# Quantising on a Trainium2 core: two bit operations in one VectorE pass, and a maximum moved to GpSimd

## What is computed

```
def fp4_quant_dequant(x):                       # BLOCK = 16
    scale = max(max(abs(block)) / 6, 1e-12)
    xn = block / scale
    idx = searchsorted([0.25, 0.75, 1.25, 1.75, 2.5, 3.5, 5.0], abs(xn))
    return [0, 0.5, 1, 1.5, 2, 3, 4, 6][idx] * sign(xn) * scale

h = layernorm(x) * (1 + ca) + sa
x = x + ga * attention(h)
h = layernorm(x) * (1 + cb) + sb
gate, up = fp4_linear(h, w_gate), fp4_linear(h, w_up)      # 256 -> 704
x = x + gb * fp4_linear(silu(gate) * up, w_down)           # 704 -> 256
```

## Time and profile before

| | |
|---|---|
| median of 3 runs | 4182.7 us (4179.85 to 4183.4) |
| the profiled execution, its own time | 4182.51 us |
| its span in the profile | 4180.7 us |
| TensorE (PE) busy | 3731.8 us, 89% |
| VectorE (DVE) busy | 3130.8 us, 75% |
| ScalarE (ACT) busy | 1946.8 us, 47% |
| GpSimd (POOL) busy | 1196.2 us, 29% |
| mean granted TensorE clock | 0.967 of full |

### The profile page before, as it was taken

One profiled execution on the slowest core, in us unless ns is written; L12 is line 12 of the kernel. 1 busy time (PEld: TensorE's weight loads), 2 busy tenths in 40 slices (PEclk: granted clock), 3 DMA queues, 4 the chain that ended last, 5 costly groups with the idle time before them and its releaser, 6 DMA issues.

```text
span 4180.7 us, 58634 instructions
## 1 busy us (share of the span) xinstructions
PE 3731.8 (89%) x22068; PEld 1974.5 (47%) x22068; DVE 3130.8 (75%) x6125; ACT 1946.8 (47%) x3535; POOL 1196.2 (29%) x886
## 2 busy tenths in 40 slices
PE   1799999999989989999999999999999998999886
PEld 0334454454545445454544545445454544544445
DVE  7477768778786787877777786777877688776855
ACT  2255444544444554444444454454544455445441
POOL 2222314132231323223132331423224132321223
PEclk6799999999999999999999999999999999999997
DMA  2532122213122122212213122222212212212000
GB/s 76 71 57 33 39 43 45 40 34 51 30 48 45 28 46 41 49 34 46 43 29 52 34 44 46 37 41 37 51 31 52 46 25 49 41 27 45 11 15 10
DMA packets 127981, 169.89 MB, mean 41 GB/s; under 512 B 22020, under 2 KB 75988, under 8 KB 127700
## 3 DMA queue, kind: packets, MB, share of 16 engines
...
...
## 4 chain that ended last, share of the span: by engine, by line
PE 73%; DVE 13%; ACT 9%; issue 2%; SPq 1%; DMA 1%; POOL 1%; DVEq 0%; ACTq 0%; POOLq 0%
PE o_acc L635 13%; PE banks L655 10%; PE banks L619 9%; PE banks L753 8%; PE banks L730 7%; PE banks L737 7%; ACT arena L815 7%; PE banks L686 4%; PE banks L711 3%; PE banks L694 3%; PE banks L746 2%; DVE banks L1020 2%; DVE tm L993 2%; PE banks L622 1%; PE banks L671 1%
## 5 line engine op out<-in xcount | busy, mean ns | idle before, releaser
L815 ACT ACTIVATE arena<-banks 128x512 f32<-128x512 f32 (+1 forms) x2432 | 1289.4, 576 | 1239.7 <-PE banks L622 702.9
L1020 DVE CUSTOM_DVE_ANT_0 banks<-banks,mask 128x640 f32<-128x640 f32 (+3 forms) x1024 | 1038.0, 1040 | 228.1 <-PE banks L655 218.3
L619 PE MATMUL banks<-qa,ka 105*128 105x512 bf16 (+3 forms) x3072 | 852.3, 332 | 154.3 <-ACT arena L815 125.4
L655 PE MATMUL banks<-ka,qa 102*128 102x512 bf16 (+3 forms) x3072 | 761.6, 334 | 104.7 <-DVE top L1020 80.1
L635 PE MATMUL o_acc<-arena,va 128*17 128x512 f32 (+3 forms) x6144 | 642.4, 500 | 13.1 <-ACT arena L815 12.5
L619 PEld LDWEIGHTS banks<-qa,ka 105*128 105x128 bf16 x3072 | 280.2, 98 | 674.1 <-ACT arena L815 471.2
L655 PEld LDWEIGHTS banks<-ka,qa 102*128 102x128 bf16 x3072 | 267.1, 99 | 484.8 <-DVE top L1020 150.9
L1018 DVE TENSOR_REDUCE top<-banks 128x2 f32<-128x768 f32 (+3 forms) x384 | 391.6, 1043 | 138.5 <-PE banks L660 107.8
L937 POOL TENSOR_TENSOR hid<-hid,tm 128x704 f32<-128x704 f32 x128 | 214.7, 1678 | 900.1 <-DVE hid L994 900.1
L753 PE MATMUL banks<-wdT,hqT 128*128 128x256 f32 x1536 | 371.2, 393 | 3.6 <-ACT hqT L846 3.2
L730 PE MATMUL banks<-wguT,xqT 128*128 128x352 f32 x1024 | 337.0, 463 | 2.8 <-ACT hqT L846 2.0
...
## 6 DMA issues: line engine op xcount, KB each, us to landing
...
```

The lines of the kernel that those rows point to most:

```text
L619: mm = pe.matmul(ps[:, m * w:(m + 1) * w], ka[g][0:KT, h, kt * P:(kt + 1) * P], qa[g][0:KT, h, q0:q0 + w], start=heads < G, stop=heads == ...
L655: mm = pe.matmul(ps[:, at:at + z - a], qa[g][0:KS, h0 + m, qt * P:(qt + 1) * P], ka[g][0:KS, h0 + m, a:z], start=qt > 0, stop=qt == 0 or h ...
L815: nc.scalar.activation(probs[:, s % P_SLOTS, j * heads:(j + 1) * heads, 0:w], ps[:, 0:heads * w].rearrange("p (h q) -> p h q", h=heads), A ...
L1020: nc.vector.tensor_tensor_reduce(out=ps, in0=ps, in1=mask[:, S - w:S], scale=1.0, scalar=MASKED, op0=ALU.add, op1=ALU.max, accum_out=tops) ...
```

## The change

The constant m gets another form. The mask 0x40800000 keeps one bit of the exponent that says "2 or more" and its lowest bit; or-ing 0x0B400000 makes of them MAGIC * 2 for magnitudes of 2 to 4, MAGIC * 4 for 4 to 8, and a tiny number below 2. The greater of that and MAGIC is what L993 made before. VectorE no longer runs L993: the maximum is the first half of the pass that adds m, which becomes a scalar_tensor_tensor. GpSimd gets a pass of its own that takes the maximum (L937 after the change), and then the two that it had (L939 and L942). Scales are made negative, so that the difference is taken as m minus the tile. In SM, the two passes that were a tensor_scalar and a copy become scalar_tensor_tensors with a second input of zeros. The planned costs of SM, XQ and HQ change with them.

```
--- before.py
+++ after.py
@@ -237,7 +237,7 @@
                 last = ("PE", ("S", b, g, j))
                 n += heads * w
             old = ("MT", b, g - 1) if g else ("MT", b - 1, NG - 1)
-            p.add("DVE", ("SM", b, g), 1.5, due, ("DVE", ("S", b, g, NT - 1)), ("DVE", old))
+            p.add("DVE", ("SM", b, g), 0.85, due, ("DVE", ("S", b, g, NT - 1)), ("DVE", old))
             older = ("TOP", b, g - 2) if g >= 2 else ("TOP", b - 1, g + 2)
             pe(("MT", b, g), 0.1, due, ("DVE", ("SM", b, g)), ring="D", on="DVE", takes_cost=0.27, then=(("SP", older),))
             p.add("SP", ("TOP", b, g), 0.8, due - 30.0, ("DVE", ("MT", b, g)), lag=4.0)
@@ -294,8 +294,8 @@
             p.add("DVE", ("LN", b, r), 2.6, due, ("DVE", ("LR", b)), ("SP", ("FROW", b)), ("PE", ("XT", *pair(-2))),
                   ("DVE", ("HQ", *tile(2 * r - 3))))
             p.add("DVE", ("XR", b, r), 1.35, due + 2, ("DVE", ("LN", b, r)), ("DVE", ("XQ", *pair(-1))))
-            p.add("DVE", ("XQ", b, r), 2.75, due + 4, ("DVE", ("XR", b, r)), ring="Q")
-            p.add("POOL", ("XQ", b, r), 2.6, due + 6, ("DVE", ("XQ", b, r)), takes="Q")
+            p.add("DVE", ("XQ", b, r), 2.1, due + 4, ("DVE", ("XR", b, r)), ring="Q")
+            p.add("POOL", ("XQ", b, r), 3.15, due + 6, ("DVE", ("XQ", b, r)), takes="Q")
             pe(("XT", b, r), 0.55, due + 8, ("POOL", ("XQ", b, r)), ("PE", ("UP", *tile(2 * r - 3))),
                ring="A", on="ACT", takes_cost=0.59)
             for t in (2 * r, 2 * r + 1):
@@ -308,8 +308,8 @@
                 pe(("UP", b, t), 2.4, late + 2, ("PE", ("GA", b, t, 1)), ("PE", ("UP", *tile(t - 1))), ring="D", on="DVE",
                    takes_cost=0.95, banks=2, then=(("ACT", ("GA", b, t, 1)),))
                 p.add("DVE", ("HR", b, t), 1.75, late + 4, ("DVE", ("UP", b, t)), ("DVE", ("HQ", *tile(t - 1))))
-                p.add("DVE", ("HQ", b, t), 3.15, late + 6, ("DVE", ("HR", b, t)), ring="Q")
-                p.add("POOL", ("HQ", b, t), 3.4, late + 8, ("DVE", ("HQ", b, t)), takes="Q")
+                p.add("DVE", ("HQ", b, t), 2.6, late + 6, ("DVE", ("HR", b, t)), ring="Q")
+                p.add("POOL", ("HQ", b, t), 4.15, late + 8, ("DVE", ("HQ", b, t)), takes="Q")
                 for k in range(2):
                     pe(("HT", b, t, k), 0.55 if k == 0 else 0.3, late + 12, ("POOL", ("HQ", b, t)),
                        ("PE", ("HT", b, t, 0)) if k else None, ("PE", ("DN", *tile(t - 2))), ring="A", on="ACT",
@@ -391,7 +391,7 @@
         mv, rs = ([sb(f"{n}{k}", shape) for k in range(2)] for n, shape in (("mv", [P, T, 2]), ("rs", [P, T])))
         ve, tn = sb("ve", [P, T]), sb("tn", [P, T])
         top = sb("top", [P, G * T])
-        top_rest = sb("top_rest", [P, G * T])
+        top_rest, zeros = sb("top_rest", [P, G * T]), sb("zeros", [P, G * T])
         top_parts = sb("top_parts", [P, 3, G * T], BF16)
         topT = [sb(f"topT{n}", [3 * G * T, P], BF16) for n in range(2)]
         rden = [sb(f"rden{n}", [P, T, G]) for n in range(2)]
@@ -934,8 +934,10 @@
                         u = (xb if kind == "XQ" else hid)[e[2] % 2][:, 0:w]
                         m, sc = tm[turn][:, 0:w], scales[kind[0]][e[2] % 2][:, :]
                         pool.wait_ge(rounded, done)
-                        nc.gpsimd.tensor_tensor(u, u, m, ALU.subtract).then_inc(gridded, 1)
-                        pool.wait_ge(gridded, done)
+                        nc.gpsimd.tensor_scalar(m, m, MAGIC, 1.0, ALU.max, ALU.mult).then_inc(gridded, 1)
+                        pool.wait_ge(gridded, 2 * done - 1)
+                        nc.gpsimd.tensor_tensor(u, m, u, ALU.subtract).then_inc(gridded, 1)
+                        pool.wait_ge(gridded, 2 * done)
                         blocks = u.rearrange("p (n k) -> p n k", k=BLOCK)
                         nc.gpsimd.tensor_tensor(blocks, blocks, sc.unsqueeze(2).broadcast_to((P, w // BLOCK, BLOCK)),
                                                 ALU.mult).then_inc(quant_done, 1)
@@ -981,24 +983,24 @@
             def block_scales(src, am, sc, iv):
 
                 step(nc.vector.tensor_reduce(am, blocks(src), AX.X, ALU.max, apply_absolute_value=True))
-                step(nc.vector.scalar_tensor_tensor(out=sc, in0=am, scalar=1.0 / 6.0, in1=tiniest[:, 0:am.shape[-1]],
-                                                    op0=ALU.mult, op1=ALU.max))
+                step(nc.vector.scalar_tensor_tensor(out=sc, in0=am, scalar=-1.0 / 6.0, in1=tiniest[:, 0:am.shape[-1]],
+                                                    op0=ALU.mult, op1=ALU.min))
                 step(nc.vector.reciprocal(iv, sc))
 
             def round_to_grid(u, iv, m):
 
-                step(nc.vector.scalar_tensor_tensor(out=blocks(u), in0=blocks(u), scalar=BELOW, in1=spread(iv),
+
+                step(nc.vector.scalar_tensor_tensor(out=blocks(u), in0=blocks(u), scalar=-BELOW, in1=spread(iv),
                                                     op0=ALU.mult, op1=ALU.mult))
-                step(nc.vector.tensor_scalar(m.bitcast(U32), u.bitcast(U32), 0x7F800000, None, ALU.bitwise_and))
-                step(nc.vector.tensor_scalar(m, m, 1.0, MAGIC, ALU.max, ALU.mult))
-                return nc.vector.tensor_tensor(u, u, m, ALU.add)
+                step(nc.vector.tensor_scalar(m.bitcast(U32), u.bitcast(U32), 0x40800000, 0x0B400000, ALU.bitwise_and, ALU.bitwise_or))
+                return nc.vector.scalar_tensor_tensor(out=u, in0=m, scalar=MAGIC, in1=u, op0=ALU.max, op1=ALU.add)
 
             def quantise(tile, n):
                 nb = n // BLOCK
                 m, am, sc, iv = tm[0][:, 0:n], amax["H"][:, 0:nb], scales["H"][0][:, 0:nb], inv["H"][:, 0:nb]
                 block_scales(tile, am, sc, iv)
                 step(round_to_grid(tile, iv, m))
-                step(nc.vector.tensor_tensor(tile, tile, m, ALU.subtract))
+                step(nc.vector.scalar_tensor_tensor(out=tile, in0=m, scalar=MAGIC, in1=tile, op0=ALU.max, op1=ALU.subtract))
                 return nc.vector.tensor_tensor(blocks(tile), blocks(tile), spread(sc), ALU.mult)
 
             def run():
@@ -1021,12 +1023,15 @@
                                                            op0=ALU.add, op1=ALU.max, accum_out=tops).then_inc(d_free, 1)
                     elif kind == "SM":
                         dve.wait_ge(d_free, in_d["S", b, e[2], NT - 1])
-                        step(nc.vector.tensor_scalar(top_parts[:, 0, :], top[:, :], -1.0, None, ALU.mult))
-                        step(nc.vector.scalar_tensor_tensor(out=top_rest[:, :], in0=top[:, :], scalar=-1.0, in1=top_parts[:, 0, :],
+                        part = [top_parts[:, n, :] for n in range(3)]
+                        step(nc.vector.scalar_tensor_tensor(out=part[0], in0=top[:, :], scalar=-1.0, in1=zeros[:, :],
+                                                            op0=ALU.mult, op1=ALU.add))
+                        step(nc.vector.scalar_tensor_tensor(out=top_rest[:, :], in0=top[:, :], scalar=-1.0, in1=part[0],
                                                             op0=ALU.mult, op1=ALU.subtract))
-                        step(nc.vector.tensor_copy(top_parts[:, 1, :], top_rest[:, :]))
-                        nc.vector.tensor_tensor(top_parts[:, 2, :], top_rest[:, :], top_parts[:, 1, :],
-                                                ALU.subtract).then_inc(top_ready, 1)
+                        step(nc.vector.scalar_tensor_tensor(out=part[1], in0=top_rest[:, :], scalar=1.0, in1=zeros[:, :],
+                                                            op0=ALU.mult, op1=ALU.add))
+                        nc.vector.scalar_tensor_tensor(out=part[2], in0=top_rest[:, :], scalar=1.0, in1=part[1],
+                                                       op0=ALU.mult, op1=ALU.subtract).then_inc(top_ready, 1)
                     elif kind == "MT":
                         g = e[2]
                         if g >= 2:
@@ -1136,7 +1141,8 @@
             step(nc.vector.memset(slope_row[:, 7, 1:6:2], 1.0))
             dve.sem_inc(tiny_set, 1)
             nc.vector.memset(va[:, :, :, HD:VW], 1.0)
-            nc.vector.memset(tiniest[:, :], 1e-12)
+            nc.vector.memset(tiniest[:, :], -1e-12)
+            nc.vector.memset(zeros[:, :], 0.0)
             step(nc.vector.memset(o_acc[:, :], 0.0))
 
             dve.wait_ge(pool_set, 4)
```

47 lines of the change are left out of this document (26 added, 21 removed).

## The result

The changed kernel takes 4264.1 us (median of 4, 4260.69 to 4268.89), beside 4181.27 us for the kernel before on the same chip. The ratio is 1.020, interval 1.018 to 1.022: about 2% slower. The forecast was 4151 us, with a range of 4112 to 4200.

The account below looks back on a forecast made before the run. TensorE, busy 89% of the span, was taken as the main bound, with waits for VectorE partly winnable. From 4182.5 us, terms of -22 - 5 + 0 + 1 - 3.5 - 2 + 0 = -31.5 us gave 4151 us, range 4112 to 4200.

Parts of the forecast that it names:

- term 4: GpSimd's added pass: 0.72 and 0.52 us each, mostly hidden behind attention work, bare in the tail: +1 us.
- Terms 1, 2: VectorE loses L993: -22 us where it collides with GpSimd's splittings, -5 us in the other 164 quantisations.
- term 5: Weights quantised ahead of the loop: eight tiles lose a pass of 0.3 to 0.53 us while TensorE waits: -3.5 us.
- Term 6: SM's two passes given a second input were to collide less with GpSimd: between 0 and -8 us, taken as -2.
- the two single places: Two quantisations beside GpSimd splittings in a batch: removing L993 was to win 0.44 us in one, 1.13 in the other.
- I take all of it: The mean win of 0.8 us at 28 collisions, -22 us, counted in full towards the kernel's time.
- rival B: TensorE is the bound: VectorE's freed time turns idle, only the weights' 3.5 us stay; 4179 us, chance 0.17.
- Term 7: New planned costs move GpSimd's splittings of units 2 and 3 in the lists: about 0, bounds -41 and +55 us.
- Rival C: Unit 2's splitting, moved ahead of tile 2, stalls VectorE's rounding there every batch, a third collision: 4206 us, chance 0.17.
- The signs to look for: Profile checks: GpSimd's new pass near 0.72 and 0.52 us, its busy time 1330 to 1340, maxima waits about 55 us.

Follow-up runs that it names:

- the run with the addition: The changed kernel with m's constant formed so that GpSimd's new pass adds MAGIC instead of taking the maximum, same lists: 4136.0 us, ratio 0.989.
- the lists with room: The changed kernel with GpSimd's planned costs raised from 3.15 and 4.15 to 4.55 and 6.05 us: 4102.3 us; with the addition instead of the maximum: 4121.0 us.

## Why the prediction was wrong

**The step that failed is term 4.** It priced GpSimd's new pass at the rate of a tensor_scalar in the trace, L901: 0.72 and 0.52 us. That row multiplies twice; the new pass takes a maximum. Measured were 2.57 and 1.92 us. The bound from above, the two-input pace of 1.67 us, was too low as well, because I held two inputs to be the slow end of what GpSimd does. 192 passes took 451 us, where the sum had 141 with the gaps. In place of the term's +1 us, the maximum cost 128 us under these lists. The term also said that the delay hides "where TensorE has attention work in front of the transpose". With some 0.3 us of delay, that of the run with the addition, it was so: TensorE's waits for the last GpSimd pass were 56 us there, 46 before. With 2.1 us a tile they were 215.

**Terms 1, 2, 5 and 6**, with a fast pass under the lists of the change, gave 4134.6 and 4136.0 us, where 4151 was forecast with its own range of 4130 to 4172. But the agreement is partly luck. Under the lists of before, which the rows were read from, the same instructions won 4 us and not 31. The working of the two single places was right, 0.46 and 1.28 us won where I had 0.44 and 1.13. What failed is "I take all of it". In the second place the passes of LN right behind take the same turns, and lose what the rounding won: 11.61 us with them before, 11.62 after. What the first place won left TensorE waiting elsewhere, 22 us behind L1051 and the unchanged 125 us for the exponentials. That is rival B, under those lists. The weights' 3.5 us of term 5 are there: TensorE's waits for them (L590 and L600, behind L1002, now L1004) fell from 49.6 to 45.9 us, in the changed kernel and in both runs with the addition. Term 6 was -2 us and measured nothing (ratio 1.000).

VectorE's busy time was to fall by 110 to 150 us. It fell by 53 in the changed kernel and by 55 in the run with the addition. The removed pass took 144 us with it, but the bit and the rounding pass together grew from 298 to 365 us in the changed kernel: the turns went over to them. That L996 would still collide, as the prediction had it, was thus right. In every profile of the changed instructions its longest took about 2.5 us or more, where it takes 0.69 or 0.89 undisturbed. The Trainium skill has that rule in "SBUF — State Buffer", section "Who interferes with whom": a VectorE instruction with two SBUF inputs contends with a GpSimd instruction that reads SBUF. These traces agree.

**Term 7**, the lists, was 0 with bounds of -41 and +55, and measured +7 with the instructions of before. Rival C's place is in the trace of after. VectorE, tile 2, and the splitting beside it:

```profile
2213.84 2.34 DVE L995 TENSOR_SCALAR tm<-hid 128x704 uint32<-128x704 uint32 x1
2216.21 1.61 DVE L996 SCALAR_TENSOR_TENSOR hid<-tm,hid 128x704 f32<-128x704 f32 x1
```

```profile
2212.02 1.05 POOL L901 TENSOR_SCALAR parts<-xa 128x1024 bf16<-128x1024 f32 x1 [5.68 <-ACT xa L829]
2213.15 2.64 POOL L903 TENSOR_TENSOR xa<-xa,parts 128x1024 f32<-128x1024 f32 x1
2215.89 1.20 POOL L905 TENSOR_SCALAR parts<-xa 128x1024 bf16<-128x1024 f32 x1
```

The bit pass takes 2.34 us and the rounding 1.61, 2.5 us over their own time. So the third collision came, but it did not decide: the run with the addition has the same 2.34 and 1.61 us in that place and took 4136.0 us. What I missed is larger: what a pass costs depends on the lists, far beyond collisions. The same maximum cost 195 us over the addition under the lists of before, 128 under those of the change, and -19 under those with room. Reading where four jobs of GpSimd moved does not give that.

**The signs to look for** told it at once. GpSimd's new pass took over 1.5 us, the sign that term 4 is wrong; its busy time was 1667 us, not 1330 to 1340; and TensorE's waits for the maxima fell further than forecast while the time rose.

Why is the maximum faster than the addition under the lists with room (4102 against 4121)? Not by its waits: they come to 383 and 376 us. TensorE's busy time is 28 us shorter, at a higher granted clock. In the same stretch of the steady part (columns as the earlier trace rows; the maximum first, then the addition) the clock is 1.00 and 0.98, so with the addition it was in part at the lower of its two levels, 1.2 in place of 2.4 GHz:

```profile
1000.00:2000.00 1000.00, 932.46 (x5641) 498.54 (x5639) 771.06 (x1464) 499.99 (x906) 417.98 (x269) 1.00 0.24 43
```

```profile
1000.00:2000.00 1000.00, 932.52 (x5604) 499.87 (x5604) 774.01 (x1465) 492.43 (x894) 333.64 (x266) 0.98 0.24 42
```

Left open is why the clock stayed up with the one and not with the other.
